# A fused attention and mixture-of-experts layer: dispatch of the tokens by groups of 512 into fixed expert regions, instead of one dispatch for all 2048

## The reference

```python
mod = (silu(c) @ wmod).reshape(2, 6, 1, -1)          # sa, ca, ga, sb, cb, gb
h = layernorm(x) * (1 + ca) + sa
x = x + ga * attention(h)                            # 16 heads of 8, causal, then @ W_o
h = layernorm(x) * (1 + cb) + sb
logits = relu(h @ Wr1 + br1) @ Wr2 + br2             # router: 128 -> 32 -> 8
tg, ti = top_k(softmax(logits), 2)
tg = softmax(tg / 2)
out = silu(h @ Ws1 + bs1) @ Ws2 + bs2                # shared expert: 128 -> 512 -> 128
for e in range(8):                                   # all f32
    out += sum(tg * (ti == e)) * (silu(h @ We1[e] + be1[e]) @ We2[e] + be2[e])
x = x + gb * out
```

## Time and profile before

| | us |
|---|---|
| median of 3 runs | 483.80 |
| fastest, slowest | 482.98, 485.03 |
| span of the profiled execution | 482.4 |
| attention, from the start to the last value product | 310.6 |
| from there to the first expert up product | 30.2 |
| expert loop, to the last expert down product | 121.3 |
| from there to the end of the span | 20.3 |

### The profile page before, as it was taken

How to read it: one execution, slowest core, us unless ns; L and a number is a source line. 1 busy time by engine, 2 the same in 40 slices (tenths; PEclk the granted TensorE clock), 3 DMA queues, 4 the chain that set the end, 5 groups by cost and what they waited for, 6 DMA issues and landing times.

```text
span 482.4 us, 9071 instructions
## 1 busy us (share of the span) xinstructions
PE 419.0 (87%) x2974; PEld 246.1 (51%) x2974; DVE 319.8 (66%) x1143; ACT 268.0 (56%) x614; POOL 140.4 (29%) x234
## 2 busy tenths in 40 slices
PE   4689899899999999999999998998668778989870
PEld 3344333534435345345344343447568568878860
DVE  5687998888889888878878815368624333534527
ACT  3353657657677575755847676464245544443723
POOL 2170530100101102502501001020757664666420
PEclk9999999999999999999999999999979995999995
DMA  4334030250302103003000057000111110112144
GB/s 140 100 112 129 36 93 10 61 172 1 93 10 57 47 1 87 15 2 95 7 1 24 1 180 193 24 22 2 52 37 45 44 46 27 40 46 44 34 136 148
DMA packets 21307, 29.09 MB, mean 60 GB/s; under 512 B 3876, under 2 KB 15381, under 8 KB 20757
## 3 DMA queue, kind: packets, MB, share of 16 engines
q1 hardware_dynamic: 18333, 23.01, 15.8%
q0 software_dynamic: 2496, 5.12, 3.8%
q10 hardware_dynamic: 432, 0.39, 0.3%
HBM read 20.44 MB, written 7.80 MB: 59 GB/s over the span
## 4 chain that ended last, share of the span: by engine, by line
PE 69%; DVE 11%; issue 7%; ACT 5%; DMA 3%; another core or an unknown queue 2%; SPq 1%; POOL 0%; DVEq 0%; POOLq 0%; ACTq 0%
PE oacc L1546 14%; PE sc L1526 11%; PE mx L1497 10%; PE sc L1817 8%; PE oacc L1828 8%; PE sc L1531 2%; DVE masked L1121 2%; PE mx L1555 2%; ACT osb L777 2%; PE sc L1629 2%; DVE mxp L1125 2%; ACT pr L886 1%; DMA S<-q_parts 1%; PE mx L1649 1%
## 5 line engine op out<-in xcount | busy, mean ns | idle before, releaser
L768 ACT ACTIVATE pr<-sc 128x512 f32<-128x512 f32 (+1 forms) x304 | 157.1, 581 | 90.6 <-PE sc L1531 50.4
L1121 DVE CUSTOM_DVE_ANT_0 masked<-mx,later 128x128 f32<-128x128 f32 (+3 forms) x256 | 111.6, 485 | 13.1 <-PE mx L1497 12.3
L1497 PE MATMUL mx<-S 72*128 72x512 bf16 (+3 forms) x384 | 111.7, 328 | 8.9 <-DMA S<-q_parts 2.2
L1526 PE MATMUL sc<-S 75*128 75x512 bf16 (+3 forms) x384 | 110.6, 328 | 0.6 <-ACT pr L768 0.3
L1125 DVE TENSOR_REDUCE mxp<-mx 128x1 f32<-128x512 f32 x128 | 82.6, 685 | 23.9 <-PE mx L1497 23.3
L1546 PE MATMUL oacc<-pr,vb 128*32 128x512 f32 (+3 forms) x768 | 74.4, 501 | 0.0
L886 ACT ACTIVATE pr<-sc,bcur 128x128 f32<-128x128 f32 x156 | 44.4, 369 | 42.9 <-PE sc L1817 23.5
L1526 PEld LDWEIGHTS sc<-S 75*128 75x128 bf16 x384 | 35.3, 97 | 47.6 <-issue 24.1
L1497 PEld LDWEIGHTS mx<-S 72*128 72x128 bf16 x384 | 34.1, 97 | 49.4 <-DVE mxp L1121 14.8
L1828 PE MATMUL oacc<-vb,pr 128*128 128x128 f32 x312 | 46.0, 294 | 10.6 <-ACT pr L886 10.3
L1817 PE MATMUL sc<-S,vb 128*128 128x128 f32 x312 | 44.6, 289 | 10.6 <-issue 10.1
(11 more groups left out here) (247 smaller groups left out, 469.3 us busy)
## 6 DMA issues: line engine op xcount, KB each, us to landing
S<-q_parts SPq DMA_DIRECT2D x48, 96.0 KB
S<-k_parts SPq DMA_DIRECT2D x21, 192.0 KB
S<-in_we SPq DMA_DIRECT2D x1, 2048.0 KB, 9.4
S<-in_we SPq DMA_DIRECT2D x4, 512.0 KB, 10.1
parts<-token_results SPq DMA_DIRECT2D x4, 512.0 KB, 5.3
x_sb<-in_x SPq DMA_DIRECT2D x4, 256.0 KB, 4.1
hidden_rows<-parts SPq DMA_DIRECT2D x4, 256.0 KB, 2.4
out_y<-attn SPq DMA_DIRECT2D x4, 256.0 KB, 2.3
```

Of the source, the lines that this page charges most:

```text
L768: act.activation(pr[:, group % NBUF, h:h + n, at:at + w], src, ACT.Exp, scale=float(DK) ** -0.5).then_inc(s["exp_done"], 1)
L1121: ins = dve.tensor_tensor_reduce(masked[:, d % 2, w * m:w * m + w], mx[:, a % RING, w * m:w * m + w], later[:, HALF - w:HALF], 1.0, LOWEST ...
L1497: ins = pe.matmul(dst[:, w * m:w * m + w], S3[0:CROSS, r3, 1, q:q + P], S3[0:CROSS, r3, 0, kk:kk + w], start=(m == 0), stop=True, skip_gro ...
L1526: ins = pe.matmul(dst[:, w * m:w * m + w], S3[0:CROSS + 3, r3, 0, kk:kk + P], S3[0:CROSS + 3, r3, 1, q:q + w], start=(m == 0), stop=True, ...
```

## The change

**Places.** Each expert has a fixed region of 2048 slots in a DRAM array `slot_rows` (with 8 more blocks at the end). As soon as a group's experts are chosen, PE sums the choices of that group alone (unit `pf`, 5 products), and DVE adds a running count (`carry`): that gives the row addresses of the group's 1024 chosen rows (`slots_of`). POOL sends them with 8 indirect DMAs, of 129 numbers a row: 128 channels and the place of its result. The sends of group 0 stand beside units of task 5, those of group 1 beside task 6; those of 2 and 3 follow behind their `pf`.

**Blank rows.** As a tile may hold slots without a token, the whole array is filled first: POOL clears a buffer, and ACT issues nine DMAs, one every 5 units from unit 110 (task 2, unit 34) to unit 150, eight of 1.06 MB from 16 partitions each (each partition's 8256 bytes written to 8 places), and one of 0.53 MB. `hidden_rows` of groups 0 and 1 waits for all nine, since the buffer is the same.

**Tiles.** Three lists of tiles (9, 8 and 22) are made by DVE (`tile_list`, 17 instructions) as groups come in: the first holds full tiles of groups 0 and 1, the second adds group 2, the third the rest. SP loads the rows of a tile (66 KB) from the address in the list, up to 12 tiles ahead; POOL's gathers are gone. The copy of the turned rows goes from DVE to ACT, and the copy of the result from ACT to DVE, where it adds the expert's second bias. The bias products, the turning of gates and the comparisons are gone; the gates' exponentials stand behind the loop.

**Order.** Behind the last unit come one shared up product, `pf` of group 2, the two halves of the output and the first expert tile. The steps of group 3 stand in tiles 0 to 5, its `pf` in tile 6; two shared up products a tile stand in tiles 0 to 6, one in tile 7, and one piece of the shared down products a tile in tiles 16 to 31. The useless small products behind the attention are gone, and PSUM banks of these units are given by the function `unit_banks`.

```diff
+        (5, 0): ("pf", 0, 0),
...
+        (6, 0): ("pf", 1, 0),
...
+TILES = [9, 8, 22]
+FIRST_TILE = [0, 9, 17]
+ROUTED = 39
+FIRST_DOWN = 16
+CHAIN = {0: ("at",), 1: ("wo",), 3: ("x2t",), 4: ("rt",), 5: ("lg",)}
+BLANK_AT, FILL_AT, FILL_EVERY, FILLS = (2, 24), 34 + 2 * 38, 5, 9
+SEND_LAG, SEND_EVERY = 3, 2
...
-    order += [(kind, 3, h) for kind in ("half", "at", "wo", "x2t", "rt", "lg") for h in range(2)]
+    order += [UPS[0], ("pf", 2, 0), ("half", 3, 0), ("half", 3, 1), ("begin", 0, 0)]
+    for i in range(ROUTED):
+        order.append(("head", i, 0))
+        order += [(kind, 3, h) for kind in CHAIN.get(i, ()) for h in range(2)]
+        if i == 6:
+            order.append(("pf", 3, 0))
+        if 2 * i + 1 < len(UPS):
+            order += UPS[2 * i + 1:2 * i + 3]
+        if 0 <= i - FIRST_DOWN < len(DOWNS):
+            order.append(DOWNS[i - FIRST_DOWN])
+        if i == ROUTED - 4:
+            order.append(("odds", 0, 0))
+        order.append(("tail", i, 0))
...
-        hd = nc.dram_tensor("hidden_rows", [TOK, C], F32, kind="Internal").ap()
...
+        xd = nc.dram_tensor("slot_rows", [(NE * REGION + 8) * P, ROWW], F32, kind="Internal").ap()
...
-                             (wr2_sb[32:33, :], br2), (be2_sb[0:NE, :], be2), (be2_sb[NE:NE + 1, :], bs2),
+                             (wr2_sb[32:33, :], br2),
+                             (be2_sb[:, :, :], be2.unsqueeze(0).broadcast_to([P, NE, C])),
+                             (bs2_sb[:, :], bs2.broadcast_to([P, C])),
...
+            def load_rows(i):
+                phase = max(p for p in range(3) if FIRST_TILE[p] <= i)
+                if i == FIRST_TILE[phase]:
+                    sp.wait_ge(s["list_ready"], phase + 1)
+                    for g in range((0, 2, 3)[phase], phase + 2):
+                        sp.wait_ge(sent[g], 16 * 8)
+                if i >= XR:
+                    sp.wait_ge(y_stored[(i - XR) % ROWS], 16 * ((i - XR) // ROWS + 1))
+                at = sp.value_load(tile_r[0:1, i:i + 1], min_val=0, max_val=P * (NE * REGION + 7))
+                sp.dma_start(xrow[:, i % XR, :], xd[bass.ds(at, P), :]).then_inc(rows_in[i % XR], 16)
...
+                chained(pool.memset(blank[:, :, :], 0.0))
+                pool.iota(blanki[:, :, C], pattern=[[1, 24]], base=2 * TOK,
+                          channel_multiplier=24).then_inc(s["blank_ready"], 1)
...
+                if g < 2:
+                    pool.wait_ge(s["filled"], 16 * FILLS)
+                else:
+                    pool.wait_ge(sent[g - 2], 16 * 8)
+                chained(pool.tensor_tensor(own[:, :, 0, 0:C], xn[:, tiles, :],
+                                           rowm[:, 1, b:b + 1, :].broadcast_to([P, 4, C]), ALU.mult))
+                pool.iota(rowski[:, g % 2, :, :, C], pattern=[[2, 4], [1, 2]], base=8 * g, channel_multiplier=2 * NT)
+                chained(pool.tensor_tensor(own[:, :, 1, 0:C], own[:, :, 0, 0:C],
+                                           rowm[:, 0, b:b + 1, :].broadcast_to([P, 4, C]), ALU.add))
+                pool.tensor_tensor(own[:, :, 0, 0:C], own[:, :, 0, 0:C],
+                                   rowm[:, 0, b:b + 1, :].broadcast_to([P, 4, C]), ALU.add)
+                pool.tensor_tensor(x_sb[:, tiles, :], x_sb[:, tiles, :],
+                                   bg[:, b:b + 1, :].broadcast_to([P, 4, C]), ALU.add).then_inc(s["h2_ready"], 1)
+            def send(g, n, k):
+                if n == 0 and k == 0:
+                    pool.wait_ge(s["rowi_ready"], g + 1)
+                    pool.wait_ge(s["h2_ready"], g + 1)
+                pool.indirect_dma_start(xd, bass.IndirectOffsetOnAxis(ap=rowi[:, g, k, n:n + 1], axis=0),
+                                        rowsk[:, g % 2, n, k, :], None).then_inc(sent[g], 16)
+            def scatter(i):
+                pool.wait_ge(s["y_done"], i + 1)
+                pool.indirect_dma_start(yd, bass.IndirectOffsetOnAxis(ap=xrow[:, i % XR, C:C + 1].bitcast(I32), axis=0),
+                                        yst[:, i % ROWS, :], None).then_inc(y_stored[i % ROWS], 16)
...
-            def gather(i):
-                if i >= FREE:
-                    pool.wait_ge(s["xt_ready"], i - FREE + 1)
-                pool.indirect_dma_start(xrow[:, i % FREE, :], None, hd,
-                                        bass.IndirectOffsetOnAxis(ap=inv[:, i:i + 1], axis=0)
-                                        ).then_inc(rows_in[i % FREE], 16)
...
-            pool.wait_ge(s["inv_ready"], 1)
-            pool.wait_ge(s["h2_out"], 64)
-            for i in range(ROUTED + YLAG):
-                if i < ROUTED:
-                    gather(i)
-                if i == YLAG:
-                    pool.wait_ge(s["goal_ready"], 1)
-                if i >= YLAG:
-                    scatter(i - YLAG)
...
+            def x_copy(i):
+                act.wait_ge(s["xt_ready"], i + 1)
+                act.activation(xTg[:, i % 2, :], mx[:, 1 + i % 2, 0:P], ACT.Copy).then_inc(s["xt_done"], 1)
...
+            def fill_slots(m):
+                act.wait_ge(s["blank_ready"], 1)
+                if m < NE:
+                    dst = xd[SLOTS * m:SLOTS * m + SLOTS, :].rearrange("(j u r) c -> u j (r c)", u=16, r=16)
+                    src = blank[16 * m:16 * m + 16, 0:16, :].rearrange("p r c -> p (r c)")
+                    act.dma_start(dst, src.unsqueeze(1).broadcast_to([16, 8, 16 * ROWW])).then_inc(s["filled"], 16)
+                else:
+                    act.dma_start(xd[SLOTS * NE:SLOTS * NE + 8 * P, :].rearrange("(p r) c -> p r c", r=8),
+                                  blank[:, 16:24, :]).then_inc(s["filled"], 16)
...
+                    if at >= FILL_AT and (at - FILL_AT) % FILL_EVERY == 0 and (at - FILL_AT) // FILL_EVERY < FILLS:
+                        fill_slots((at - FILL_AT) // FILL_EVERY)
...
+            def choose(g):
+                ns = slice(4 * g, 4 * g + 4)
+                chained(dve.tensor_copy(topf[:, ns, :], topi[:, ns, 0:2]))
+                chained(dve.tensor_tensor(sel[:, g], iota8[:, :].unsqueeze(1).unsqueeze(1).broadcast_to([P, 2, 4, NE]),
+                                          topf[:, ns, :].rearrange("p n k -> p k n").unsqueeze(3).broadcast_to([P, 2, 4, NE]),
+                                          ALU.is_equal))
+                dve.tensor_tensor(chosen[:, NE:].rearrange("p (n e) -> p n e", e=NE), sel[:, g, 0], sel[:, g, 1],
+                                  ALU.add).then_inc(s["chosen_ready"], 1)
+            def slots_of(g, a):
+                if g == 0:
+                    dve.wait_ge(s["tile_ready"], 1)
+                dve.wait_ge(s["aux_ready"], a + 1)
+                pfx = unit[a][:, 0:5 * NE].rearrange("p (n e) -> p n e", e=NE)
+                chained(dve.tensor_tensor(place[:, :, :], pfx[:, 0:4, :], carry[:, :].unsqueeze(1).broadcast_to([P, 4, NE]),
+                                          ALU.add))
+                dve.tensor_tensor(carry[:, :], carry[:, :], pfx[:, 4, :], ALU.add).then_inc(s["aux_free"], 1)
+                chained(dve.tensor_tensor(place1[:, :, :, :], place[:, :, :].unsqueeze(1).broadcast_to([P, 2, 4, NE]), sel[:, g],
+                                          ALU.mult))
+                chained(dve.tensor_reduce(place[:, 0, :].rearrange("p (k n) -> p k n", k=2), place1[:, :, :, :], AX_X, ALU.add))
+                dve.tensor_copy(rowi[:, g], place[:, 0, :].rearrange("p (k n) -> p k n", k=2)).then_inc(s["rowi_ready"], 1)
+                dve.wait_ge(s["rowi_ready"], g + 1)
...
+            def tile_list(p, part):
+                n, at = TILES[p], FIRST_TILE[p]
+                if part == 0:
+                    half = (1 - P) / (2 * P) if p < 2 else (P - 1) / (2 * P)
+                    chained(dve.tensor_scalar(full_e[:, :], carry[:, :], 1.0 / P, half, ALU.mult, ALU.add))
+                    chained(dve.tensor_scalar(full_e[:, :], full_e[:, :], ROUND, -ROUND, ALU.add, ALU.add))
+                    chained(dve.tensor_tensor(more_e[:, :], full_e[:, :], at_e[:, 0:NE], ALU.subtract))
...
+            def y_out(i):
+                dve.wait_ge(s["dn_ready"], i + 1)
+                if i >= ROWS:
+                    dve.wait_ge(y_stored[i % ROWS], 16 * (i // ROWS))
+                dve.tensor_tensor(yst[:, i % ROWS:i % ROWS + 1, :], oacc[:, i % 2:i % 2 + 1, 0:P],
+                                  be2_sb[:, bass.ds(experts[i], 1), :], ALU.add).then_inc(s["y_done"], 1)
...
+            def prefix(g, a):
+                pe.wait_ge(s["chosen_ready"], g + 1)
+                ring_free(a)
+                pfx = unit[a][:, 0:5 * NE]
+                pe.matmul(pfx, ones[:, :], chosen[:, :], start=True, stop=True)
+                pe.matmul(pfx[:, 0:4 * NE], upper[:, :], chosen[:, NE:], start=False, stop=True, skip_group_check=True)
+                for d in range(2, 5):
+                    ins = pe.matmul(pfx[:, NE * d:], ones[:, :], chosen[:, NE:NE * (6 - d)], start=False,
```

(50 more changed lines are left out.)

725 lines of the change are left out of this document (277 added, 448 removed).

## The result

The changed kernel takes 516.4 us (510.23 to 518.12) against 483.4 for the kernel before (481.94 to 485.03), run beside it: a ratio of 1.065, with an interval of 1.057 to 1.073. The forecast was 463 us, in a range of 449 to 488.

The account below looks back on a forecast made before the run. PE was taken as the bound, busy 419.0 of 482.4 us. 482.4 - 22.2 + 19.5 - 23.2 + 4 = 460.5; runs' median 1.4 above gives 461.9, called 463 us as bounds lie more above; 8-in-10 range 449 to 488.

Parts of the forecast that it names:

- 1, the start of the loop: From the last value product to the first expert up product: no wait for group 3's router and whole dispatch, -22.2 us.
- 2, PE's work in the loop: Expert loop: PE's full-clock work rises from 85.2 to 104.7 us, +19.5 us, moved from ahead of and behind the loop.
- 3, stalls: Expert loop: time that isn't full-speed PE work falls from 36.1 to 12.9 us with the gathers gone, -23.2 us.
- 4, the attention: Attention: 33 added DVE instructions cost 3 us, DMA issues on ACT 0.5, the bias load 0.5; sum +4 us.
- The fills: Attention, from 144.6 us: nine fills, 8.98 MB, cost nothing if done by 208, before POOL's `hidden_rows` delays PE.
- The rule of 141 GB/s: Fills in the attention: the rate that decides whether they end by 208 us, 63.5 us after their start.
- the rival with 0.20: Attention: few partitions make fills slow; at 78 GB/s they end at 260, POOL, then PE, stall 52 us: 515; chance 0.20.
- 5, the tail: Behind the loop: same chain of results, gates' exponentials beside the last scatter and reload; 0 us, from -1.5 to 1.5.

## Why the prediction was wrong

**1, the start of the loop: right.** -21.8 against -22.2, by the path that was forecast.

**2, PE's work in the loop: right.** On the chip without holes the loops differ by 19.5 us (114.3 and 94.8), where 19.5 was forecast.

**3, stalls: right cause, one step wrong.** Stalls were to fall from 36.1 to 12.9 us, and fell to 126.5 - 104.7 = 21.8. The gathers caused 30 of the 36, as argued. But the step "POOL has only 39 scatters and 16 sends in the loop" took the sends for harmless, although they are indirect DMAs of POOL like the gathers: they cost 12 us; without them stalls are 114.0 - 104.7 = 9.3.

**4, the attention: wrong, twice.** "Between 0 and 6.9 I take 3" for DVE's instructions was low: a row of 22 between the maxima costs 6.7 us, more than their own time, since PE idles and its clock falls; group 0's cost 1.2 us. And the sends beside units weren't priced at all: 7 us where they stand, on a chip with holes. Together 15 us where 4 were forecast.

**The fills: the step that failed and decided.** "So the fills cost nothing if done by 208" is the step: its condition was met, if barely (first issue at 145.5, last landing at 207.9, so 144 GB/s against the 141), and still they cost 31 us. The rule of 141 GB/s asked only when the instruction that waits for the fills would be released. It left out the loads of k and q, which wait for no fill and share the DMA engines. The same four products on PE, before and after:

```profile
176.58 0.40 PE L1497 MATMUL mx<-S 72*128 72x128 bf16 x4
```

```profile
206.92 0.59 PE L1520 MATMUL mx<-S 72*128 72x128 bf16 x4 [14.90 <-DMA S<-q_parts]
```

Before, the load's issue ends at 157.2, a slack of 19.4 us to its use at 176.6; the rows of the prediction don't hold this load, and no rival was made of it. That the rival with 0.20 ended near the measured time (515) is chance: its mechanism, POOL held up, didn't occur, nor did its slow fills, which were to end at 231 to 260. Few partitions are some 13 of the 31 us (31.2 against 18.4), the rest is the closeness of so many bytes, as far as one pair shows; and halved in size, spread over 128 units instead of 40 and taken from all partitions, they cost nothing that can be measured. The three were changed at once there, and no run parts them.

**5, the tail: right.** 20.4 against 20.3.

## What to carry to other kernels

Bulk transfers that nothing waits for must be priced by what they hold up: find the next load on any queue, its issue and its need, and ask what rate is left to it. Here neither all partitions alone (18 us left) nor distance alone (15 us left) was enough, small pieces with both were. Where indirect DMAs of POOL are suspected of stalls, the ones that the change adds count as well as those that it removes: here 39 gathers cost 30 us of the loop, and the sends put 12 us back. And measure on the chip at hand, as the loop of the kernel before took 121.3 us on one and 94.8 on another. Work moved from a gap into a dense loop gains only what stood empty in the gap: here 2 of 22 us (-21.8 and +19.5), and the rest has to come from stalls that the change really removes.

## What the runs showed of the hardware

- DMAs from 16 partitions filled the DMA engines' time (share 1.02) at 106 GB/s, from 128 partitions half of it (0.53) at 191 GB/s, with the same pieces of 8256 bytes. Nine loads queued from another engine meanwhile took 29.3 us to issue instead of 5.5.
- On the chips that run the kernel before in 482 to 484 us, PE's semaphores arrived late, 5.6 us among POOL's indirect gathers (347.79 to 353.36) and 7.5 at the end of a row of sends (413.95 to 421.43); beside scatters of results alone they didn't. Without gathers the kernel before fell from 484.1 to 453.1 us. On the other chip, with the same gathers, no update in the loop was late, and the kernel before took 460.0. The mechanism is open.
